# A graph layer on one core: every fifth group's x turned in 32x32 blocks on VectorE, and selections as one-source operations

## What is computed

```python
msg = relu(x[src] + edge_attr)
agg = segment_sum(msg, dst, num_segments=50000)
h = x + agg
h = relu(relu(h @ W1 + b1) @ W2 + b2)      # W1: 128x256, W2: 256x128
out = layernorm(x + h, axis=-1)
```

## Time and profile before

| | us |
|---|---|
| median of 3 runs | 459.13 |
| lowest, highest | 459.03, 459.8 |
| the profiled execution, its own time | 459.26 |
| its span | 457.8 |

### The profile page before, as it was taken

One profiled execution on the slowest core, in us unless ns is written; L12 is line 12 of the kernel. 1 busy time (PEld: TensorE's weight loads), 2 busy tenths in 40 slices (PEclk: granted clock), 3 DMA queues, 4 the chain that ended last, 5 costly groups with the idle time before them and its releaser, 6 DMA issues.

```text
span 457.8 us, 10674 instructions
## 1 busy us (share of the span) xinstructions
PE 449.9 (98%) x3046; PEld 379.9 (83%) x3046; DVE 434.0 (95%) x1760; ACT 394.7 (86%) x930; POOL 368.5 (80%) x402
## 2 busy tenths in 40 slices
PE   7999999999999999999999999999999999999995
PEld 6888888888888888888888888888888888888884
DVE  6899999999999999999999999999999999999997
ACT  3599888898888889988888888888888888888886
POOL 7777888888888878768888888888888888888842
PEclk9999999999999999999999999999999999999999
DMA  5586666666666666666666666666666666666632
GB/s 133 163 235 200 192 193 202 196 195 199 187 197 188 193 199 202 183 192 203 197 200 189 201 195 197 186 201 196 200 196 197 188 196 202 189 197 198 195 126 90
DMA packets 83870, 86.82 MB, mean 190 GB/s; under 512 B 12023, under 2 KB 79508, under 8 KB 83812
## 3 DMA queue, kind: packets, MB, share of 16 engines
q1 hardware_dynamic: 75044, 68.77, 48.5%
q0 software_dynamic: 8496, 17.38, 13.8%
q10 hardware_dynamic: 272, 0.00, 0.0%
HBM read 60.51 MB, written 25.60 MB: 188 GB/s over the span
## 4 chain that ended last, share of the span: by engine, by line
PE 97%; DMA 1%; DVE 1%; ACT 0%; issue 0%; DVEq 0%
PE h_ps L1059 38%; PE h1T_ps L1051 36%; PE hT_ps L972 11%; PE hT_ps L967 9%; DMA x_src<-in_x_dram,first_pairs 1%; DMA first_pairs<-in_pairs_dram 0%; PE hT_ps L943 0%; DVE stats L702 0%; PE hT_ps L960 0%; DVE z L695 0%; PE h1T_ps L1039 0%; ACT std L858 0%; ACT h1T L853 0%; PE h1T_ps L1032 0%; PE h_ps L1025 0%
## 5 line engine op out<-in xcount | busy, mean ns | idle before, releaser
L135 POOL DMA_INDIRECT x_src<-in_x_dram,src_of x254 | 269.4, 1061 | 66.7 <-issue 59.6
L1059 PE MATMUL h_ps<-w_sb,h1T 128*128 128x128 f32 x1564 | 197.6, 276 | 0.0
L1051 PE MATMUL h1T_ps<-hT,w_sb 128*128 128x384 f32 x520 | 188.6, 486 | 0.0
L1059 PEld LDWEIGHTS h_ps<-w_sb,h1T 128*128 128x128 f32 x1564 | 185.2, 192 | 0.0
L853 ACT ACTIVATE h1T<-h1T_ps,b_sb 128x384 f32<-128x384 f32 (+1 forms) x262 | 151.4, 579 | 35.2 <-PE h1T_ps L1051 26.9
L1051 PEld LDWEIGHTS h1T_ps<-hT,w_sb 128*128 128x128 f32 x520 | 88.9, 191 | 34.1
L872 ACT ACTIVATE y<-z,shift,rstd 128x128 f32<-128x128 f32 x263 | 114.6, 483 | 1.1 <-DVE shift L722 0.2
L602 POOL TENSOR_SCALAR y<-z,rstd,shift 128x128 f32<-128x128 f32 x123 | 87.3, 710 | 13.6 <-DVE shift L722 9.0
L972 PE MATMUL hT_ps<-sel,msg_hi 128*128 128x216 f32 x250 | 94.8, 447 | 0.0
L702 DVE BATCH_NORM_STATS2 stats<-z 128x6 f32<-128x128 f32 x391 | 88.7, 282 | 0.1
L967 PE MATMUL hT_ps<-ident,x_sb 128*128 128x128 f32 x375 | 87.6, 273 | 0.0
(11 more groups left out here) (139 smaller groups left out, 186.6 us busy)
## 6 DMA issues: line engine op xcount, KB each, us to landing
x_sb<-in_x_dram SPq DMA_DIRECT2D x130, 192.0 KB, 2.5
out_dram<-y SPq DMA_DIRECT2D x130, 192.0 KB, 2.4
pre_msg<-in_edge_attr_dram SPq DMA_DIRECT2D x130, 128.0 KB, 2.8
x_src<-in_x_dram,src_of POOLq DMA_INDIRECT x254, 3.0
w_sb<-in_w_dram SPq DMA_DIRECT2D x2, 128.0 KB
dst_rows<-in_dst_dram SPq DMA_DIRECT2D x1, 97.7 KB
x_src<-in_x_dram,first_pairs POOLq DMA_INDIRECT x6, 2.7
b_sb<-in_b_dram SPq DMA_DIRECT2D x1, 64.0 KB, 3.1
```

Source lines behind the costliest of these rows:

```text
L135: nc.gpsimd.indirect_dma_start(out=c["x_src"][:, g % EB, k, :], out_offset=None, in_=x, in_offset=bass.IndirectOffsetOnAxis(ap=index, axis ...
L1051: nc.tensor.matmul(h1T_ps[h][:, 0:n, 0:p], w1_sb[:, h * 128:(h + 1) * 128], hT[:, 0:n, 0:p], start=True, stop=True).then_inc(h1_summed, 1)
L1059: last = nc.tensor.matmul(h2_ps[g % 2][0:p, t, :], h1T[:, h, t, 0:p], w2_sb[:, h, :], start=(h == 0 and t == 0 and not biased(g, c)), stop ...
```

## The change

Three things change.

1. In the 23 groups 12, 17, ... 122 ("block groups") x is loaded a second time, by four DMAs of 32 partitions each, into `x_blocks`, so that the 32x32 blocks of a tile stand in exchanged places: partition block b of the destination takes feature block b of all node blocks. Turning every 32x32 block in itself then gives the tile's full transpose. VectorE does so in one instruction over 384 columns (`turn_blocks`, three groups ahead). For these groups TensorE makes no transposes; its first message matmul covers all 384 columns with a wide selection, so that every column is written (`sum_onto_zero`). VectorE adds the turned x to the sum on its way to SBUF (`join_hT`), which stands for ScalarE's `copy_hT`.
2. `select` makes the two windows by two one-source operations of 216 columns, each with the edge's target as a scalar for each partition, in every group that it does (all but the first three and the last two). In a block group the first is 384 columns wide, from the table of the whole group into `wide_sel`.
3. SyncE issues the four block loads four groups ahead, and waits before them until the earlier block group's x was turned.

```diff
+BLOCK = 32
+BLOCK_GROUPS = range(12, 124, 5)
+BLOCKS_AHEAD = 4
...
+def start_blocks(sp, x, g, c):
+
+    src = x[g * G:(g + 1) * G, :].rearrange("(a i t) (b j) -> b i t a j", i=BLOCK, t=T, j=BLOCK)
+    for b in range(128 // BLOCK):
+        sp.dma_start(c["x_blocks"][b * BLOCK:(b + 1) * BLOCK, :, :, :], src[b, :, :, :, :]).then_inc(c["blocks_loaded"], 16)
...
             if g > 0 and inside(g + X_AHEAD):
                 load_x(g + X_AHEAD)
+            if block_turned(g + BLOCKS_AHEAD):
+                if blocks_to(g + BLOCKS_AHEAD) > 1:
+                    sp.wait_ge(blocks_turned, blocks_to(g + BLOCKS_AHEAD) - 1)
+                start_blocks(sp, x, g + BLOCKS_AHEAD, c)
...
-                nc.vector.tensor_tensor(sel[:, g % EB, :, :], node_in_range[:, :, :].to_broadcast([128, K, T * WP]),
-                                        dst_of[:, g - FIRST_ROW:g - FIRST_ROW + 1, :].rearrange("p a k -> p k a").to_broadcast([128, K, T * WP]),
+                if block_turned(g):
+                    nc.vector.tensor_scalar(wide_sel[:, :], c["node_in_group"][:, :], dst_of[:, g - FIRST_ROW, 0:1], None, ALU.is_equal)
+                else:
+                    nc.vector.tensor_scalar(sel[:, g % EB, 0, :], node_in_range[:, 0, :], dst_of[:, g - FIRST_ROW, 0:1], None, ALU.is_equal)
+                nc.vector.tensor_scalar(sel[:, g % EB, 1, :], node_in_range[:, 0, :], dst_of[:, g - FIRST_ROW, 1:2], None,
                                         ALU.is_equal).then_inc(sel_ready, 1)
+
+        def turn_blocks(g):
+
+            dve.wait_ge(c["blocks_loaded"], 16 * (128 // BLOCK) * blocks_to(g))
+            nc.vector.transpose(xT[:, :], c["x_blocks"][:, :, :, :].rearrange("p t a j -> p (t a j)")).then_inc(blocks_turned, 1)
+
+        def join_hT(g):
+
+            dve.wait_ge(blocks_turned, blocks_to(g))
+            dve.wait_ge(hT_summed, g + 1)
+            nc.vector.tensor_tensor(hT[:, 0:T, :], hT_ps[:, 0:T, :], xT[:, :].rearrange("p (t q) -> p t q", t=T),
+                                    ALU.add).then_inc(hT_copied, 1)
...
             if inside(g - 2) and g < END:
                 reciprocal(g - 2)
+            if block_turned(g + 2):
+                join_hT(g + 2)
             statistics(g)
...
                 add_edge_attr(g + 3)
+            if block_turned(g + 3):
+                turn_blocks(g + 3)
...
-            if inside(g + 1):
+            if inside(g + 1) and not block_turned(g + 1):
                 copy_hT(g + 1)
...
+        def sum_onto_zero(g):
+
+            def add(k, part, stop=False):
+                tile = wide_sel[:, :] if k == 0 else sel[:, g % EB, k, :]
+                cols = tile.rearrange("p (t q) -> p t q", t=T)[:, :, 0:WP]
+                return nc.tensor.matmul(hT_ps[:, 0:T, LO[k]:LO[k] + WP], part[:, g % EB, k, :], cols,
+                                        start=False, stop=stop, skip_group_check=True)
+
+            pe.wait_ge(sel_ready, g - FIRST_GROUPS + 1)
+            pe.wait_ge(msg_hi_ready, parts_to(g, c) + 1)
+            nc.tensor.matmul(hT_ps[:, 0:T, :], msg_hi[:, g % EB, 0, :], wide_sel[:, :].rearrange("p (t q) -> p t q", t=T),
+                             start=True, stop=False, skip_group_check=True)
+            add(1, msg_hi)
+            pe.wait_ge(msg_lo_ready, parts_to(g, c) + 1)
+            add(0, msg_lo)
+            add(1, msg_lo, stop=True).then_inc(hT_summed, 1)
```

More of the change, by code:

```diff
@@ L124, in start_x, with block_turned, blocks_to @@
     sp.dma_start(c["x_sb"][0:partitions(g, c), slot, 0:tiles(g, c), :], rows(x, g, c)).then_inc(c["x_loaded"][slot], 16)
+def block_turned(g):
+    return g in BLOCK_GROUPS
+def blocks_to(g):
+    return sum(block_turned(i) for i in range(g + 1))
+def start_blocks(sp, x, g, c):
+    src = x[g * G:(g + 1) * G, :].rearrange("(a i t) (b j) -> b i t a j", i=BLOCK, t=T, j=BLOCK)
+    for b in range(128 // BLOCK):
+        sp.dma_start(c["x_blocks"][b * BLOCK:(b + 1) * BLOCK, :, :, :], src[b, :, :, :, :]).then_inc(c["blocks_loaded"], 16)
 def start_edge_attr(sp, edge_attr, g, first, c):
@@ L515, in main_path @@
     targets_ready = sem("targets_ready")
+    blocks_turned = sem("blocks_turned")
+    wide_sel = sb("wide_sel", [128, T * 128], FP32R)
+    xT = sb("xT", [128, T * 128])
     sum_ready = sem("sum_ready")
@@ L694, in add_x @@
                 h2_of = h2[:, g % 2, :, :]
+            if block_turned(g):
+                dve.wait_ge(x_loaded[g % XB], (g // XB + 1) * 16)
             nc.vector.scalar_tensor_tensor(z[0:p, g % ZB, 0:n, :], h2_of[0:p, 0:n, :], 0.0, x_sb[0:p, g % XB, 0:n, :],
@@ L1092, in main_tensor @@
             hidden_sum(g)
-            if g + 1 < END:
+            if block_turned(g + 1):
+                sum_onto_zero(g + 1)
+            elif g + 1 < END:
                 sum_turned(g + 1)
@@ L1410, in gnn_resnorm_kernel @@
             x_sb=sb("x_sb", [128, XB, T, D]),
+            x_blocks=sb("x_blocks", [128, T, 128 // BLOCK, BLOCK]),
+            blocks_loaded=sem("blocks_loaded"),
             ea_loaded=[sem(f"ea_loaded{u}") for u in range(EB)],
```

## The result

The changed kernel takes 475.94 us (median of 4 runs, 474.76 to 476.92), the kernel before 459.08 (4 runs, 458.85 to 459.80): ratio 1.0362, 95% interval 1.0347 to 1.0376. Slower was forecast, with 470.5 us in a range of 457 to 487; the loss is 16.9 us where 11.5 was expected. The profiled execution has a span of 474.7 us, 16.9 over the span of before.

A forecast was written before the change was run, and what follows sets the result against it. TensorE was taken as the bound, VectorE close behind. With VectorE behind after each block, five groups take 17.40 for 16.90 us: +0.50 times 23 is +11.5 on 459.26, 470.8, or 470.5 against the median; range 457 to 487.

The forecast's parts named there:

- What bounds the kernel: TensorE bounds the kernel before, with a period of 3.38 us a group; VectorE needs 3.11, so 0.27 slack.
- TensorE's term: In a block group, three transposes less and a wider matmul save TensorE 0.26 us, 6.0 us over 23.
- the rival in which it comes through: VectorE's slack holds the additions, msg_hi's wait stays under 0.1, TensorE's saving reaches the end: 453 us, chance 0.11.
- VectorE's terms: VectorE's costs: selection pair 0.50 us; in block groups wide selection 0.09 more, transpose 0.48, join 0.48, sum 1.05.
- The rival of cheap selections: Selection pairs cost near 0.35 us, so VectorE recovers between blocks: 461 us, chance 0.14.
- By place it doesn't fit: Work queued behind the join on VectorE makes msg_hi 0.47 us late for TensorE, though 1.05 fits 1.35 slack on average.
- The price of the place: Each block group saves TensorE 0.26 us and makes it wait 0.5 in the next: +0.24, 5.5 us over 23.
- The deadline: TensorE wants msg_hi 2.33 us after the start of h_ps.
- the 2.80 at which msg_hi was to end: Behind a join, pre_msg starts 1.89 us after h_ps and msg_hi ends 0.91 later, at 2.80.
- the third rival: GpSimd and VectorE's selections hold each other up, 0.1 to 0.4 us a group; chance 0.20 with a half-rate transpose, beyond 480.
- VectorE doesn't recover wholly: VectorE, behind after a block, needs 3.26 to 3.35 us a group, catching up only 0.03 to 0.12 before the next.
- Loads and queues cost nothing: SyncE's block loads, GpSimd's later gathers (at most 0.5 us) and ScalarE's dropped copy are hidden, costed at nothing.

The follow-up runs named there:

- e7_tensor_only: Changed kernel with TensorE's saving alone: no blocks loaded, turned or joined, ScalarE copies the sum, x left out in block groups; 454.64 us, ratio 0.9880.
- e8_copy_not_join: Changed kernel with blocks loaded and turned on VectorE but no join; ScalarE copies the sum, turned x left out; 457.49 us, ratio 0.9948.
- e13_relief: e12_fewer_stats with, in that iteration, also one tile aggregated and the first selection left out, 0.78 us less in all; 457.81 us, ratio 0.9973.
- e9_every_tenth: Changed kernel with 12 block groups ten apart for 23 five apart; 466.79 us, ratio 1.0157.
- e12_fewer_stats: Changed kernel with VectorE making statistics of one tile for three in the iteration with the join, 0.40 us less; 463.73 us, ratio 1.0091.
- e14_tenth_apart: Changed kernel with 12 blocks ten apart, turn seven groups ahead, edge sums and msg_lo earlier, shift and selections directly behind the join; 463.54 us, ratio 1.0091.
- e2_blocks_only: Changed kernel with its block groups, but the other groups keep the two-source selection of the kernel before; 476.85 us, ratio 1.0387.
- e4_loads_only: Changed kernel with the new selections and block loads, VectorE waiting for them, but nothing turned or joined, TensorE transposing as before; 459.26 us, ratio 1.0001.
- e1_sel_only: Changed kernel with the new selections in every group and no block groups; 459.0 us, ratio 0.9992.

## Why the prediction came out as it did

**What bounds the kernel, and TensorE's term**: right. 0.24 us a block group for 0.26; e7_tensor_only gives 454.6 for the 453 of the rival in which it comes through.

**VectorE's terms**: right to 0.02 us. The pair of selections 0.48 (0.50), the wide one 0.09 more (0.09), the turn 0.49 (0.48), the join 0.47 (0.48), all from start to start. The changed kernel's operations that had no row before, as durations (ns, least/median/most):

```profile
L680 DVE STREAM_TRANSPOSE xT<-x_blocks x23: 562/566/572, 49.0 to 436.5; 128x384 f32<-128x384 f32 x23
L686 DVE TENSOR_TENSOR hT<-hT_ps,xT x23: 556/558/559, 51.1 to 438.5; 128x384 f32<-128x384 f32 x23
L674 DVE TENSOR_SCALAR sel<-node_in_range,dst_of x105: 315/323/519, 62.5 to 429.1; 128x216 fp32r<-128x216 f32 x105
```

The rival of cheap selections (0.35 a pair) is refuted by 0.48.

**By place it doesn't fit**: right, and it is the cause. e8_copy_not_join and e13_relief show it from two sides: take the join away, or some 0.78 us of work from behind it, and the group behind the block has its 3.38 again.

**The price of the place** is the term that was mis-sized: "+0.24 a block, the least", measured 0.53 (e9_every_tenth). The deadline held nearly: msg_hi is wanted 2.33 after the start of h_ps. It ended 2.46, 2.61 and 3.02 after it in e12_fewer_stats, e14_tenth_apart and e9_every_tenth, so 0.13, 0.28 and 0.69 late, and what was lost before its piece was 0.19, 0.34 and 0.75, each time 0.06 more. What failed is the 2.80 at which msg_hi was to end. In e9_every_tenth, from start to start as the prediction counts: the join starts 0.09 after h_ps and not 0.03 (+0.06); the join takes 0.48 as expected; statistics and shift take 0.64 for 0.66 (-0.02); the selections 0.69 for 0.50 (+0.19); the aggregates 0.21 for 0.22 (-0.01). So pre_msg starts at 2.11 and not at 1.89 (+0.22), and from there to the end of msg_hi it is 0.91, as expected. The rest of the gap, 0.07, is that the loss is 0.08 more than the lateness (0.77 for 0.69) where 0.03 was taken (0.50 for 0.47), and 0.02 less of TensorE's saving.

The 0.19 is the third rival in small. GpSimd's gather and the second selection meet behind a join: in the changed kernel this selection is stretched 20 times in 23 blocks and nowhere else, in e9_every_tenth 9 times in 12 blocks. The join releases the gather and so sets its start. Where the selection starts 0.15 us into the gather (e12_fewer_stats), or is the two-source one (e2_blocks_only), it isn't stretched, and by e2_blocks_only it costs TensorE 0.15 us a block, some 3.5 of the 16.9 us as an estimate. The prediction had this gather "at most 0.5 us later, with four groups to spare", which holds for who waits for the gather, and missed what it meets on its new date. The Trainium skill, "SBUF — State Buffer", section "Who interferes with whom", has an instruction of VectorE in a two-port mode and one of GpSimd exclude each other for a whole instruction. Here the selection was held for 0.2 us of a gather's 0.98, and one that began 0.04 us ahead of a gather wasn't held, as the next rows, of e14_tenth_apart, show:

```profile
292.12 0.33 DVE L673 TENSOR_SCALAR sel<-node_in_range,dst_of 128x216 fp32r<-128x216 f32 x1
292.36 0.35 DVE L674 TENSOR_SCALAR sel<-node_in_range,dst_of 128x216 fp32r<-128x216 f32 x1
...
292.40 0.98 POOL L155 DMA_INDIRECT x_src<-in_x_dram,src_of  x1 [0.44 <-DVE hT L686]
```

So no run here shows a lock as long as the instruction.

**VectorE doesn't recover wholly**: right in sign, and smaller. It is worth 0.12 a block, 3.26 for 3.14, against 0.53 for the place. The forecast itself, 17.40 for five groups, came near the measured 17.55 in part by luck: it is the sum of a VectorE that bounds every group. In fact TensorE runs at its own 3.38 in three groups of five, and nearly all of the loss lies in the two periods at a block. The late msg_hi was priced at 0.24 net where it costs 0.53; a VectorE that doesn't recover was priced at 0.26 more (0.50 less 0.24) where it costs 0.12. The second error hides part of the first.

**Loads and queues cost nothing**: right for the loads. x_sb takes 3.2 us to land, for 2.5, in e4_loads_only too, which loses no time. The later gather did cost, as said above.

Not settled: why the four blocks in the stretch with the checks cost 0.3 us more each. It fits VectorE's extra work there, and wasn't tried.

## What to carry to other kernels

Slack added up over groups (1.35 us in five) is no cover for work that comes in one piece: what counts is how late the engine's next result may be at that place, here some 0.6 us of delay (pre_msg starts 0.80 after h_ps, and could start at 1.42, since msg_hi ends 0.91 after it and is due at 2.33), and what is queued between the new operation and that result. A result that TensorE takes as weights is due before TensorE is free: one which came 0.18 to 0.03 us ahead of that cost 0.19 to 0.34 us here. And an operation that releases a GpSimd transfer sets its date; look at what VectorE does while the transfer is issued, here 0.5 us after its start.

## What was not expected of the hardware

- A piece whose weights come late: with msg_hi 0.18 us ahead of the moment at which TensorE was free, 0.19 us were lost, with 0.03 us ahead 0.34, with 0.38 us behind it 0.75. All three give a loss that begins 0.37 us ahead of that moment.
- A one-source selection of VectorE that begins about 0.5 us into an indirect DMA of GpSimd mostly takes longer, 0.52 us for 0.32 (216 columns; 20 of 23 in the changed kernel, 9 of 12 in e9_every_tenth), while the 23 that began about 0.3 us into one kept 0.33; in e1_sel_only one that began 0.36 us into it took 0.67. msg_lo took 0.54 for 0.42 where it began 0.56 us into one. A two-source selection that ran over the same place kept its 0.60 (e2_blocks_only). An edge sum that began 0.13 us into GpSimd's tensor_scalar took 0.60 for 0.39.
- A transpose of 32x32 blocks of fp32 over 128x384 elements costs 0.49 us on VectorE from start to start, as much as an addition from PSUM over as many.
